# A decoder kernel whose first self attention gets half-row transposes and masks, fewer PSUM banks, its layer normalisation on ScalarE and its sine product on GpSimd

## The chip, the cores and the metric

The kernel runs on one core of one Trainium2 chip. The metric is device microseconds of one execution; the time of a kernel is the median of its runs.

## The reference, cut to what matters

A decoder of four layers runs over 32 sequences of 128 tokens and 128 features. The change touches only the first self attention of the first layer. What it computes, for x of 32 x 128 x 128:

```python
q, k = x @ W_Q + b_Q, x @ W_K + b_K            # 32 heads of 32
v = x @ W_V + b_V                              # 256 heads of 1: 8 per attention head
q, k = x_rot * cos + flip(x_rot) * sin         # rotary, over all 32 dimensions of a head
s = [virtual_k ; k] . q / sqrt(32)             # 16 virtual keys in front of 128, causal
p = softmax(s)
z = p @ [virtual_v ; v]
x = layernorm(x + z @ W_O)
```

`flip(a, b) = (-b, a)` swaps the halves of a head.

## The kernel before, in words

`l0_attn` (from L161) works in rounds. A round n handles eight heads of one sequence: NR = 4 rounds make a sequence, N = 128 rounds the stage. Two sequences share one projection, so eight rounds make a pair; `TAKE` lists which projections of the next pair are due in which of the eight rounds: X (the transposed input), K0 and Q0, K1, V and Q1, K2, Q2, K3, Q3. Those of the first pair run ahead of the loop (`FIRST`).

TensorE (L316 to L331) does in round n, in this order: `weights_T` (L278) for the first six of nine 128x128 blocks of round n-2's softmax weights, `scores(n)` (L260), the last three blocks, the projections due (`produce`, L237), and `mix` (L287), which multiplies the transposed weights of round n-2 with the virtual values (L298) and the values (L300). `scores` first writes the causal mask into each of four score banks, by a product of an identity with the mask in bf16 (L271), the first two banks after half of the previous round's subtractions, the other two after all of them; then it adds 8 products of 32 rows for keys and queries (L275). Every fourth round `project` (L304) runs ahead of the masks. PSUM has eight banks: 0 to 3 hold the scores, 4 and 5 form a ring that transposed weights and projections share in the order written out at `order`, and 6 and 7 hold the mixed values of two rounds each, in turn (`z_of`).

VectorE (L484 on) does the softmax's maximum (L458), every fourth round the residual (L453), the values once in a pair (L440), and the subtractions (L467, L471). Behind them come in even rounds `normalise` (L482), in odd rounds `spread` (L476), and in some rounds `turn` (L447), the product of the half-swapped keys and queries with the sine. Every 16 rounds the layer normalisation of four sequences follows: statistics (L68, L72) and two rounds later `dve_ln_scale` (L124).

ScalarE (L388 on) copies the transposed weights to SBUF in three pieces of 384 (`weights`, L384), takes the exponential (L395), evacuates projections with their bias (`take`, L359 and L369), and inverts the softmax sums (`invert`, L375 and L377).

GpSimd (L405 on) handles a quarter q of a pair's keys and queries at a time: two products with the cosine (L422), then, when the sine product is there, two additions (L427). SP swaps the half heads with eight DMAs per quarter (L342).

Of the kernel before, what the change touches and what calls it, by code (L numbers as in the profile page):

```python
# [9 lines left out]
ALU = mybir.AluOpType  # L10
# [6 lines left out]
P = 128  # L17
# [109 lines left out]

def dve_ln_affine(nc, dve, E, s, k, src, dst, scale, shift):
# [35 lines left out]
def l0_attn(nc, E):  # L164
# [22 lines left out]
    with sublayer(nc, "cst vkc one xt_ps xt kq_ps raw flip0 flip1 cosm sinm rot v_ps v s_ps mx sub_a sub ex pt_ps pt z_ps shuf lnz rz zt o_ps res" + LN) as (s, ctx):  # L187
# [8 lines left out]
        MASK = ctx.enter_context(nc.sbuf_tensor(f"maskb_{nc.next_id()}", [P, 2, K], BF16))  # L196
# [3 lines left out]
        order = [(item, 0) for item in FIRST]  # L200
        for n in range(N + 2):
            if n >= 2:
                order += [("T0", n - 2), ("T1", n - 2), ("T2", n - 2)]
            order += due(n)
        place = {item: k for k, item in enumerate(order)}

        def ring(item, n):
            return PS[:, 4 + place[item, n] % 2, :]

        def ring_free(pe, item, n):  # L210

            k = place[item, n] - 2
            if k < 0:
                return
            before, m = order[k]
            if before[0] == "T":
                pe.wait_ge(s.pt, 3 * m + int(before[1]) + 1)
            elif before == "X":
                pe.wait_ge(s.xt, m + 1)
            elif before == "V":  # L220
                pe.wait_ge(s.v, m + 1)
            else:
                pe.wait_ge(s.raw, 8 * m + 2 * int(before[1]) + (before[0] == "Q") + 1)

        def z_of(m):
            return PS[:, 6 + m % 2, 0:2 * P].rearrange("p (r q) -> p r q", r=2)
# [6 lines left out]
        def o_of(t):  # L233
            return PS[:, 0, 384:384 + P]

        with nc.Block() as block:
            @block.tensor  # L237
            def _(pe):
                def produce(item, p):
                    bank = ring(item, p)  # L240
                    ring_free(pe, item, p)
# [17 lines left out]
                def scores(n):  # L259
# [6 lines left out]
                    if n >= 2 * NR and n % NR == 0:  # L266
                        project(n // NR - 2)
# [11 lines left out]
                def weights_T(n, c):  # L279
                    item = f"T{c}"  # L280
                    if c == 0:
                        pe.wait_ge(s.ex, n + 1)
                    ring_free(pe, item, n)
                    for q in range(3):
                        ins = nc.tensor.transpose(ring(item, n)[:, q * P:(q + 1) * P], SM[:, n % 3, 3 * c + q, :], E.ident)  # L285
                    ins.then_inc(s.pt_ps, 1)

                def mix(n, a):
                    r, t, m = n % NR, n // NR, n // 2
                    p, b = t // PB, t % PB  # L290
                    z = z_of(m)[:, r % 2]
                    pe.wait_ge(s.pt, 3 * n + 2 + a)
                    if a == 0:
                        if n % NPR == 0:
# [18 lines left out]
                for item in FIRST:  # L313
                    produce(item, 0)
                for n in range(N + NR + 1):
                    live = 2 <= n < N + 2  # L316
                    if live:
                        weights_T(n - 2, 0)
                        weights_T(n - 2, 1)
                    if n < N:  # L320
                        scores(n)
                    elif n % NR == 0:
                        pe.wait_ge(s.sub, N)
                        project(n // NR - 2)
                    if live:
                        weights_T(n - 2, 2)
# [20 lines left out]
            def _(act):  # L347
                nc.scalar.preload_act_table_set(EXP_LN)

                def take(item, p):  # L350
                    if item == "V":
                        return
                    bank = ring(item, p)
# [25 lines left out]
                def weights(k):  # L379
# [3774 lines left out]
```

## Time and profile before

| | us |
|---|---|
| median of 3 runs | 3554.46 (3548.69 to 3561.56) |
| profiled execution | 3553.89 |
| its span | 3552.0 |
| first self attention, about | 71 to 742 of the span |

Busy shares of the span: TensorE 78%, its weight loads 56%, VectorE 69%, ScalarE 55%, GpSimd 44%. The page's chain of waits covers the end of the kernel, far from the stage that changes, so the stage is read by its own windows, timelines and waits. Its reductions (L458) come once a round and serve as a clock of the rounds.

### The profile page before, as it was taken

How to read it: one execution, taken by the hardware profiler on the slowest of the kernel's cores; microseconds unless marked ns; L12 is line 12 of the kernel's file. 1: busy time of each engine (PE TensorE's matmuls, PEld its weight loads, DVE VectorE, ACT ScalarE, POOL GpSimd, SP SyncE). 2: the span in 40 equal slices, each digit the busy share in tenths (PEclk: the TensorE clock that was granted, in tenths of full speed). 3: DMA queues.
4: the chain of work that ended last, by engine and by line, in shares of the span. 5: the costliest groups of instructions: out<-in, count | busy, mean ns of one | idle time of the engine just before them, and what ended most of it. 6: DMA issues, size and time to landing. Idle time of an engine off the chain costs nothing. (4 is left out here: it accounts for less than half of the span.)

```text
span 3552.0 us, 78931 instructions
## 1 busy us (share of the span) xinstructions
PE 2759.6 (78%) x29371; PEld 1989.7 (56%) x29371; DVE 2452.4 (69%) x7164; ACT 1962.8 (55%) x3803; POOL 1547.7 (44%) x1205
## 2 busy tenths in 40 slices
PE   2899999987875957989899999956655657868956
PEld 1677777655564845656455555534433447745646
DVE  6688888865555967976676776659882544568955
ACT  2677777744443854765555655555433724556637
POOL 3554555412237823520165555623231258815544
PEclk9999999999966978989999999977767858979958
DMA  4333333212202211000000000000007012300013
GB/s 137 56 55 55 55 55 55 49 60 79 69 18 63 76 50 66 2 1 1 1 2 3 2 3 2 3 1 19 19 27 219 12 44 66 103 26 12 2 32 100
DMA packets 103272, 151.01 MB, mean 43 GB/s; under 512 B 26266, under 2 KB 76524, under 8 KB 101756
## 3 DMA queue, kind: packets, MB, share of 16 engines
q1 hardware_dynamic: 91546, 123.11, 13.9%
q0 software_dynamic: 10912, 22.70, 1.9%
q8 instruction: 237, 3.88, 0.5%
q14 instruction: 143, 1.17, 0.1%
q10 hardware_dynamic: 434, 0.15, 0.0%
HBM read 81.13 MB, written 49.04 MB: 37 GB/s over the span
## 5 line engine op out<-in xcount | busy, mean ns | idle before, releaser
L458 DVE TENSOR_REDUCE MX<-banks 128x8 f32<-128x1152 f32 x128 | 173.2, 1353 | 101.3 <-PE banks L275 101.2
L2450 POOL TENSOR_TENSOR SM<-SM,RZ 128x1232 f32<-128x1232 f32 x64 | 143.8, 2247 | 190.0 <-DVE RZ L2492 188.9
L1727 POOL DMA_INDIRECT expert_results<-Y,DST x181 | 177.8, 982 | 81.5 <-DVE DST L1910 33.8
L427 POOL TENSOR_TENSOR KT<-KT,FL 128x512 f32<-128x512 f32 x64 | 81.6, 1276 | 302.0 <-DVE FL L447 302.0
L1714 POOL DMA_INDIRECT sorted_rows<-SRC,IDX x160 | 156.7, 979 | 128.7 <-DVE IDX L1843 82.1
L1496 PE MATMUL banks<-XC,WR 128*128 128x128 f32 x1448 | 197.4, 280 | 0.3 <-ACT XC L1616 0.2
L384 ACT COPY PT<-banks 128x384 f32<-128x384 f32 x384 | 170.3, 478 | 47.3 <-PE banks L285 43.6
L2434 ACT COPY PT<-banks 77x512 f32<-77x512 f32 x256 | 143.0, 583 | 86.2 <-PE banks L2353 83.3
L285 PE MATMUL banks<-sb_c_ident,SM 128*128 128x128 f32 x1152 | 182.7, 286 | 9.8 <-ACT PT L384 9.3
L1496 PEld LDWEIGHTS banks<-XC,WR 128*128 128x128 f32 x1448 | 180.8, 196 | 2.6 <-ACT XC L1616 1.9
L2790 POOL TENSOR_TENSOR KQ<-T,EX 128x1024 f32<-128x1024 f32 x32 | 76.1, 2379 | 208.4 <-ACT EX L2771 208.4
L471 DVE TENSOR_TENSOR SM<-banks,MX 128x512 f32<-128x512 f32 x256 | 163.6, 680 | 0.0
L2353 PE MATMUL banks<-sb_c_ident,SM 128*77 128x128 f32 x1024 | 160.2, 291 | 0.1
L1506 PE MATMUL banks<-WR,HT 128*128 128x128 f32 x1008 | 149.3, 282 | 5.7 <-DVE HT L1949 3.3
L395 ACT ACTIVATE SM<-SM 128x1152 f32<-128x1152 f32 x128 | 150.4, 1175 | 4.9 <-DVE SM L471 4.2
L285 PEld LDWEIGHTS banks<-sb_c_ident,SM 128*128 128x128 f32 x1152 | 121.5, 141 | 55.8 <-issue 25.7
L2353 PEld LDWEIGHTS banks<-sb_c_ident,SM 128*77 128x77 f32 x1024 | 114.8, 151 | 53.6 <-issue 40.0
L369 ACT ACTIVATE RAW<-banks,weight_region 128x256 f32<-128x256 f32 x256 | 108.0, 477 | 63.4 <-PE banks L256 53.9
L256 PE MATMUL banks<-XT,weight_region 128*128 128x256 f32 x512 | 135.8, 395 | 4.6 <-ACT RAW L369 4.0
L1506 PEld LDWEIGHTS banks<-WR,HT 128*128 128x128 f32 x1008 | 127.1, 192 | 13.5 <-DVE HT L1949 7.4
L59 PE MATMUL banks<-sb_c_ident,x_res 128*128 128x128 f32 x256 | 47.4, 329 | 112.0 <-PEq L48 112.0
L1635 ACT ACTIVATE HT<-banks,WR 128x128 f32<-128x128 f32 x284 | 81.5, 368 | 95.7 <-PE banks L1496 91.2
(566 smaller groups left out, 8597.9 us busy)
## 6 DMA issues: line engine op xcount, KB each, us to landing
FL<-RAW SPq DMA_DIRECT2D x512, 64.0 KB, 2.3
sorted_rows<-in_zeros_dram SPq DMA_DIRECT2D x33, 528.0 KB, 8.6
XR<-sorted_rows SPq DMA_DIRECT2D x181, 66.0 KB, 1.9
SRC<-expert_results SPq DMA_DIRECT2D x16, 512.0 KB, 7.5
T<-s4d_k_dram SPq DMA_DIRECT2D x8, 1024.0 KB, 10.0
weight_region<-in_l_ffn__wall_dram SPq DMA_DIRECT2D x1, 4112.0 KB
film_dram<-F SPq DMA_DIRECT2D x8, 512.0 KB, 2.9
FO<-film_dram SPq DMA_DIRECT2D x8, 512.0 KB, 4.7
```

The source lines that it names most:

```text
L285: ins = nc.tensor.transpose(ring(item, n)[:, q * P:(q + 1) * P], SM[:, n % 3, 3 * c + q, :], E.ident)
L384: nc.scalar.copy(PT[:, n % 2, 3 * c:3 * c + 3, :].rearrange("p h q -> p (h q)"), ring(f"T{c}", n)[:, 0:3 * P]).then_inc(s.pt, 1)
L395: nc.scalar.activation(SM[:, (n - 1) % 3], SM[:, (n - 1) % 3], ACT.Exp, scale=SCALE).then_inc(s.ex, 1)
L458: nc.vector.tensor_reduce(MX[:, n % 2], sc, AXX, ALU.max).then_inc(s.mx, 1)
L471: nc.vector.tensor_tensor(main[:, h:h + 2], sc[:, h:h + 2, :, 0:P], bc(MX[:, n % 2, h:h + 2].unsqueeze(3), [P, 2, 2, P]), ALU.subtract).th ...
L1496: ins = nc.tensor.matmul(up_bank(j, c // 2)[:, (c % 2) * P:(c % 2 + 1) * P], w[:, at * P:(at + 1) * P], XC[:, j % 2, :], start=True, stop= ...
L1506: ins = nc.tensor.matmul(down_bank(j), HT[:, j % 2, c, :], w[:, c * P:(c + 1) * P], start=c == 0, stop=c == hb - 1)
L1714: nc.gpsimd.indirect_dma_start(out=rows, out_offset=bass.IndirectOffsetOnAxis(ap=IDX[:, k, t:t + 1], axis=0), in_=SRC[:, t, k, :], in_offs ...
L1727: nc.gpsimd.indirect_dma_start(out=results, out_offset=bass.IndirectOffsetOnAxis(ap=DST[:, j % ST:j % ST + 1], axis=0), in_=Y[:, j % ST, : ...
L2353: ins = nc.tensor.transpose(bank_of("T", k)[0:L, c * P:(c + 1) * P], SM[:, t % 3, 4 * c + a, :], E.ident)
L2434: nc.scalar.copy(PT[:, t % 2, a].rearrange("p c q -> p (c q)"), bank_of("T", k)[0:L, :]).then_inc(s.pt, 1)
L2450: nc.gpsimd.tensor_tensor(SM[:, t % 3], SM[:, t % 3], bc(RZ[:, t % 2, :].unsqueeze(2), [P, H, L]), ALU.mult).then_inc(s.nm, 1)
```

## The change

- The masks and the transposes work on half rows: a transpose loads 64 partitions and streams 64 columns, 16 of them per round in place of 8 full ones, into two banks (`turned`, banks 4 and 5); the virtual keys' block stays a full transpose, into bank 7. The masks are eight products of 64x64 in place of four.
- ScalarE copies the transposed weights in one piece of 1024 and one of 128, and inverts the sums between its copies and its exponential.
- There is no ring: of the projections due the first goes to bank 7, the second to bank 4, after ScalarE's copies of the round; the next transposes wait until they are taken. `project` moves behind the scores and those copies, and writes bank 5.
- One bank holds mixed values (6), so `mix` of an even round waits for `normalise`, which moves between VectorE's reduction and its subtractions.
- The layer normalisation is applied by ScalarE (four activations with scale and shift per partition) after a small product on VectorE.
- The sine product moves from VectorE to GpSimd, between the cosine products and the additions.

```diff
+def dve_ln_shift(nc, dve, E, s, k):
+    dve.wait_ge(s.ln_rstd, k + 1)
+    nc.vector.scalar_tensor_tensor(E.ln_std[k % 8][:], E.ln_rstd[k % 8][:], -1.0, E.ln_mv[k % 8][:, :, 0], ALU.mult, ALU.mult).then_inc(s.ln_core, 1)
+def act_ln_apply(nc, act, E, s, k, src, dst):
+    shift, rstd = E.ln_std[k % 8], E.ln_rstd[k % 8]
+    act.wait_ge(s.ln_core, k + 1)
+    for b in range(GB):
+        ins = nc.scalar.activation(dst[:, b, :], src[:, b, :], ACT.Identity, bias=shift[:, b:b + 1], scale=rstd[:, b:b + 1])
...
+        turned = PS[:, 4:6, :].rearrange("p r (h q) -> p h r q", q=64)
+        turned_vk = PS[:, 7, 0:P]
+        z_bank = PS[:, 6, 0:2 * P].rearrange("p (r q) -> p r q", r=2)
...
-                        nc.tensor.matmul(PS[:, i, 0:2 * K], IDB[:], MASK[:].rearrange("p a k -> p (a k)"), start=True, stop=False)
+                        at = HALF[i % 2]
+                        for late in range(2):
+                            nc.tensor.matmul(PS[HALF[late], i, 0:2 * K], IDB[at, at], MASK[at, late].rearrange("p a k -> p (a k)"), start=True, stop=False)
...
+                def weights_T(n):
+                    pe.wait_ge(s.ex, n + 1)
+                    if n >= 1:
+                        pe.wait_ge(s.pt, 2 * n)
+                    if n + 1 >= 2 * NR and (n + 1) % NR == 0:
+                        pe.wait_ge(s.res, (n + 1) // NR - 1)
+                    new = due(n + 1) if n >= 1 else [(item, 0) for item in FIRST] + due(0) + due(1)
+                    for item, p in new[1:]:
+                        taken(pe, item, p)
+                    for k in range(8):
+                        for r in range(2):
+                            ins = nc.tensor.transpose(turned[:, k, r, :], SM[HALF[r], n % 3, 1 + k, :], E.ident[HALF[r], HALF[r]])
                     ins.then_inc(s.pt_ps, 1)
+                    for item, p in new[:1]:
+                        taken(pe, item, p)
+                    nc.tensor.transpose(turned_vk, SM[:, n % 3, 0, :], E.ident).then_inc(s.pt_ps, 1)
...
-                        if n % 2 == 0 and m >= 2:
-                            pe.wait_ge(s.zt, m - 1)
+                        if n % 2 == 0 and m >= 1:
+                            pe.wait_ge(s.zt, m)
...
                     if live:
-                        weights_T(n - 2, 0)
-                        weights_T(n - 2, 1)
+                        weights_T(n - 2)
                     if n < N:
                         scores(n)
+                    if live:
+                        pe.wait_ge(s.pt, 2 * (n - 2) + 2)
...
+                    if n >= 2 * NR and n % NR == 0:
                         project(n // NR - 2)
-                    if live:
-                        weights_T(n - 2, 2)
...
+                    nc.scalar.copy(PT[:, n % 2, 1:9, :].rearrange("p h (r q) -> p h r q", r=2), turned).then_inc(s.pt, 1)
+                    act.wait_ge(s.pt_ps, 2 * n + 2)
+                    nc.scalar.copy(PT[:, n % 2, 0, :], turned_vk).then_inc(s.pt, 1)
...
+                    pool.wait_ge(flips[q % 2], 128 * (q // 2 + 1))
+                    f = FL[:, q % 2].rearrange("p a j (b q) -> p (a j b) q", b=PB)
+                    nc.gpsimd.tensor_tensor(f, f, bc(E.sin.unsqueeze(1), [P, 8, P]), ALU.mult).then_inc(s.sinm, 1)
...
+                    if n >= 4 and n % 2 == 0:
+                        normalise((n - 4) // 2)
                     dve.wait_ge(s.mx, n + 1)
...
-                        dve_ln_scale(nc, dve, E, s, g, grp(E.x, g), grp(E.x, g))
+                        dve_ln_shift(nc, dve, E, s, g)
```

## Rows read from the trace of the kernel before

**Rows 1.** Windows: start:end us, length, busy PE, PEld, DVE, ACT, POOL, PEclk, DMA, GB/s.
```profile
300.00:400.00 100.00, 94.58 (x1094) 72.89 (x1095) 83.12 (x145) 72.82 (x148) 48.31 (x39) 1.00 0.33 54
```

**Rows 2.** Timeline, 300 to 325 us: start, length, engine, line, operation, operands, count.
```profile
299.36 1.35 DVE L458 TENSOR_REDUCE MX<-banks 128x8 f32<-128x1152 f32 x1
...
300.63 0.28 DVE L453 TENSOR_TENSOR x_res<-banks,x_res 128x128 f32<-128x128 f32 x1
...
302.22 0.41 DVE L482 TENSOR_TENSOR ZT<-banks,RZ 128x256 f32<-128x256 f32 x1
...
302.55 1.22 DVE L447 TENSOR_TENSOR FL<-FL,sb_f_sin 128x1024 f32<-128x1024 f32 x1
...
303.79 1.89 PE L256 MATMUL banks<-XT,weight_region 128*128 128x256 f32 x8
...
304.86 1.70 ACT L369 ACTIVATE RAW<-banks,weight_region 128x256 f32<-128x256 f32 x4 [0.39 <-PE banks L256]
...
308.55 1.36 DVE L458 TENSOR_REDUCE MX<-banks 128x8 f32<-128x1152 f32 x1 [1.54 <-PE banks L275]
...
308.79 1.04 PE L256 MATMUL banks<-XT,weight_region 128*128 128x256 f32 x4
...
309.67 0.38 PE L298 MATMUL banks<-PT,sb_l_attn__vv 128*128 128x128 f32 x2
...
309.99 0.65 PE L300 MATMUL banks<-PT,VZ 128*32 128x128 f32 x16
...
310.15 1.28 DVE L471 TENSOR_TENSOR SM<-banks,MX 128x512 f32<-128x512 f32 x2
...
310.56 0.88 PE L285 MATMUL banks<-sb_c_ident,SM 128*128 128x128 f32 x6
...
311.27 0.65 PE L271 MATMUL banks<-maskb,identb 128*128 128x288 bf16 x4
...
311.86 0.77 PE L275 MATMUL banks<-KT,QT 32*128 32x144 f32 x16
...
312.70 1.36 DVE L458 TENSOR_REDUCE MX<-banks 128x8 f32<-128x1152 f32 x1 [0.94 <-PE banks L275]
```

**Rows 3.** Timeline of VectorE: reductions of rounds 0, 120 and 127.
```profile
91.41 1.36 DVE L458 TENSOR_REDUCE MX<-banks 128x8 f32<-128x1152 f32 x1 [4.78 <-PE banks L275]
...
694.69 1.35 DVE L458 TENSOR_REDUCE MX<-banks 128x8 f32<-128x1152 f32 x1
...
725.68 1.36 DVE L458 TENSOR_REDUCE MX<-banks 128x8 f32<-128x1152 f32 x1 [1.53 <-PE banks L275]
```

**Rows 4.** Waits, 130 to 690 us: us in total, times, longest us.
```profile
PEld banks L275 <- issue: 27.1, 114, 0.2
...
DVE FL L447 <- DMA FL<-RAW: 21.3, 15, 2.8
```

**Rows 5.** Timeline of TensorE in a later stage with half-row transposes (L2644).
```profile
1902.89 0.71 PE L2644 MATMUL banks<-sb_c_ident,T 64*128 64x64 f32 x16
1903.53 1.09 PE L2654 MATMUL banks<-LA,sb_a_gla_sum 64*64 64x512 f32 x8
```

**Rows 6.** Groups by line and form, whole span: busy us, mean ns, idle before and releaser.
```profile
L2747 ACT COPY T2T<-banks 128x1024 f32<-128x1024 f32 x32 | 32.7, 1022 | 0.8 <-PE banks L2644 0.8
...
L2426 ACT COPY ZT<-banks 128x128 f32<-128x128 f32 x64 | 16.0, 250 | 3.1 <-PE banks L2366 3.1
...
L1660 ACT ACTIVATE x_res<-x_res,FNM,FRS 128x128 f32<-128x128 f32 x96 | 39.0, 479 | 2.5 <-DVE FNM L1987 2.5
...
L422 POOL TENSOR_TENSOR KT<-RAW,sb_f_cos 128x512 f32<-128x512 f32 x64 | 81.4, 1272 | 4.5 <-ACT RAW L369 4.5
...
L2790 POOL TENSOR_TENSOR KQ<-T,EX 128x1024 f32<-128x1024 f32 x32 | 76.1, 2379 | 208.4 <-ACT EX L2771 208.4
```

**Rows 7.** Instructions of the half-swap tile, ns min/median/max; then DMA issues, us to landing.
```profile
L342 SPq DMA_DIRECT2D FL<-RAW x512: 507/589/1892, 78.2 to 694.4; - x171
...
FL<-RAW SPq DMA_DIRECT2D x512, 64.0 KB, 2.3
```

More of the change, by code:

```diff
@@ L195, in l0_attn, with bank_of, taken @@
         RZ = sb("RZ", [P, 2, 2, P]); ZT = sb("ZT", [P, 4, 2, P])
-        MASK = ctx.enter_context(nc.sbuf_tensor(f"maskb_{nc.next_id()}", [P, 2, K], BF16))
+        MASK = ctx.enter_context(nc.sbuf_tensor(f"maskb_{nc.next_id()}", [P, 2, 2, K], BF16))
         IDB = ctx.enter_context(nc.sbuf_tensor(f"identb_{nc.next_id()}", [P, P], BF16))
         flips = (s.flip0, s.flip1)
[L200 to L221, printed above, removed]
-            else:
-                pe.wait_ge(s.raw, 8 * m + 2 * int(before[1]) + (before[0] == "Q") + 1)
-        def z_of(m):
-            return PS[:, 6 + m % 2, 0:2 * P].rearrange("p (r q) -> p r q", r=2)
+        HALF = (slice(0, 64), slice(64, 128))
+        def bank_of(item, p):
+            if p == 0:
+                return PS[:, 4 + FIRST.index(item) % 2, :]
+            return PS[:, 4 if [row for row in TAKE if item in row][0].index(item) else 7, :]
+        def taken(pe, item, p):
+            if item == "X":
+                pe.wait_ge(s.xt, p + 1)
+            elif item == "V":
+                pe.wait_ge(s.v, p + 1)
+            else:
+                pe.wait_ge(s.raw, 8 * p + 2 * int(item[1]) + (item[0] == "Q") + 1)
+        turned = PS[:, 4:6, :].rearrange("p r (h q) -> p h r q", q=64)
+        turned_vk = PS[:, 7, 0:P]
+        z_bank = PS[:, 6, 0:2 * P].rearrange("p (r q) -> p r q", r=2)
         def value_window(p, b, r, i, a):
@@ L239, in produce @@
                 def produce(item, p):
-                    bank = ring(item, p)
-                    ring_free(pe, item, p)
+                    bank = bank_of(item, p)
                     if item == "X":
@@ L312, in _ @@
                 pe.wait_ge(s.vkc, 2)
-                for item in FIRST:
+                for k, item in enumerate(FIRST):
+                    if k >= 2:
+                        taken(pe, FIRST[k - 2], 0)
                     produce(item, 0)
@@ L352, in take @@
                         return
-                    bank = ring(item, p)
+                    bank = bank_of(item, p)
                     if item == "X":
@@ L390, in _ @@
                     if live:
-                        weights(3 * (n - 2))
-                        weights(3 * (n - 2) + 1)
+                        weights(n - 2)
+                    if n >= 4 and n % 2 == 0 and (n - 4) // 2 < HALVES:
+                        invert((n - 4) // 2)
                     if 1 <= n <= N:
@@ L430, in _ @@
             def _(dve):
-                nc.vector.tensor_copy(MASK[:], bc(E.causal.unsqueeze(1), [P, 2, K]))
+                for a in range(2):
+                    nc.vector.tensor_copy(MASK[:, :, a], E.causal)
                 nc.vector.tensor_copy(IDB[:], E.ident).then_inc(s.cst, 1)
@@ L491, in _ @@
                         residual(n // NR - 2)
-                    if n >= 4 and n % 2 == 0 and (n - 4) // 2 < HALVES:
+                    if n >= N and n % 2 == 0 and (n - 4) // 2 < HALVES:
                         normalise((n - 4) // 2)
@@ L4127, in shape_constants @@
     c["f_sin"] = np.tile(np.sin(angle) * sign, (4, 1)).astype(f)
[L4128 removed]
+    c["f_causal"] = np.where(np.arange(P + 16)[None, None] <= p[:, :, None] % 64 + 64 * np.arange(2)[None, :, None] + 16, 0, -1e30).astype(f)
     same = p // 64 == q // 64
```

54 lines of the change are left out of this document (16 added, 38 removed).

## Prediction

> **What bounds the kernel now.** Only the first self attention is touched, so I read first where it lies. The windows of 100 us show TensorE busy for 94.6 of 100 us there, at a granted clock of 1.00, the 2.4 GHz level, with no other engine above 83 [rows 1]. A busy TensorE need not be the limit, so I went to the timeline of two rounds. In the round that starts with the reduction at 308.55, TensorE's groups follow each other without a gap: projection of one item 0.88 (308.79 to 309.67), virtual values 0.32, mixing 0.57, six transposes 0.71, four masks 0.59, then the scores, whose next reduction starts 0.84 after they do [rows 2]. The score banks close a second loop of the same length: reduction to end of the subtractions 2.88 (308.55 to 311.43), then 1.27 to the next reduction: 4.15 us in all. So in a plain round TensorE's order and the score banks bind together. Rounds with two projected items, an output projection or VectorE's product with the sine are longer, and the mean from the first reduction to that of round 120 is (694.69 - 91.41)/120 = 5.03 us [rows 3]. VectorE also stands still 21.3 us, 15 times, because the product with the sine waits in its queue for the half-swapped copies [rows 4]; whoever is behind it (the next reduction, hence TensorE's masks) waits too.
>
> **The change, part by part.**
> TensorE: nine full transposes cost 0.71/6 = 0.12 us each. Sixteen half ones exist elsewhere in this kernel in the same form, 64x128 loaded and 64 columns streamed: from their start to the next group it takes 0.64, and 0.71 to their last result [rows 5]. I take that row; the far bound is eight full transposes, 0.94, if the loads of the two halves did not run side by side. The remaining full transpose costs 0.12 and a change of tile shape 0.11 (that is 0.59 for four masks less four streams of 288 columns, 0.12 each), together 0.23. The eight quarter masks use four separate tiles, so four run abreast: 2 x 0.12 and 0.11 to the scores, 0.35 instead of 0.59; bounds 0.35 and 0.59. TensorE's own work in a plain round falls by about 0.45 us.
>
> But the banks are fewer: one pair of banks for the transposes, one for the mixed values instead of two. That adds two waits, and they set the new rounds.
>
> Even rounds. Mixing now waits for the normalisation of the same round, which VectorE runs behind the reduction. Loop: 1.27 (reduction until the next instruction, 299.36 to 300.63), normalisation 0.41, a hand-over of 0.05 (estimate), virtual values 0.32, mixing 0.57, half transposes 0.64, the full one 0.23, masks 0.35, scores to reduction 0.84: 4.68 us [rows 2, 5]. Every fourth round VectorE adds the residual in front, 0.20 (its 0.28 less 0.08, by which the instruction behind the reduction overlaps too): 4.88. Queued behind the waiting mixing on TensorE is the whole next round; behind the normalisation on VectorE are the subtractions.
>
> Odd rounds with one item. The score banks: 2.88, hand-over 0.05, two masks' time 0.12, change 0.11, scores 0.84: 4.00.
>
> Odd rounds with two items (K0/Q0, V/Q1). The next transposes wait until ScalarE has taken both: 0.71 transposes, hand-over 0.06, the copy of 1024 elements 1.02, of the last 128 another 0.15 (0.25 less the 0.10 by which ScalarE's instructions overlap), 0.05, projection of two items 1.89 to its end (303.79 to 305.68), ScalarE 0.88 after it (to 306.56), 0.05: 4.81 [rows 2, 6]. The unknown is the copy's stride over two banks: 1.02 by the nearest row, a contiguous copy of the same size; 1.3 as far bound, were it eight copies of 0.25 with the overlap.
>
> Eight rounds: 4.88 + 4.81 + 4.68 + 4.81 + 4.88 + 4.00 + 4.68 + 4.00 = 36.74; sixteen: 73.5.
>
> Normalisation of the layer on ScalarE, once in 16 rounds. VectorE loses its four normalising instructions, which I count as no gain of their own, since the new loops already hold only what stays. ScalarE gains four of 0.48 [rows 6], about 1.64 with overlap, and they are in front of the next round's copies. They wait for VectorE's small product, which comes after that round's subtractions and shuffle, about 3.4 us after its reduction (2.88 and two short instructions, estimate). So the copies start at 3.4 + 0.06 + 1.64 = 5.1 and end at 6.3; the output projection needs them and takes about 1.0 to its result (estimate: the 0.88 of one projected item and the end of the pipeline): 7.4 with the hand-over. The residual behind the reduction could otherwise begin at 4.00 + 1.27 = 5.3. The round grows by 2.1; bounds 0, if ScalarE had room, and 3. Sixteen rounds: 75.6.
>
> The product with the sine on GpSimd. VectorE spends 1.22 on it [rows 2], GpSimd by the nearest row of 1024 elements 2.38 (bounds VectorE's 1.22 and twice GpSimd's 1.27), so a quarter pair keeps GpSimd busy for 4 x 1.27 + 2.38 = 7.5 us [rows 6], against about 9 us between two of them. Its path: SP issues eight transfers at 0.59, landing takes 2.3, 7.0 us [rows 7], then 2.38 and two additions: 11.9 from raw values to rotated ones. The tightest deadline is the last quarter, three rounds (14.4 us) later. So it is hidden in steady state, and if that cover of 2.5 us goes, every pair of sequences pays. In the first four rounds it is not hidden: they follow GpSimd's chain, 7.5 us each, and the first starts 1.2 later. The wait for the half-swapped copies moves from VectorE's queue to GpSimd's, where only the next quarter is behind it.
>
> **Sum.** Reduction 0 to reduction 120: 3 x 7.5, then 4.81 + 4.68 + 4.00 + 4.68 + 4.00 (no output projection yet), then 7 x 75.6: 573.9 against 603.3 [rows 3], -29.4. First reduction +1.2. The last seven intervals, 31.0 before [rows 3]: 7.0 + 4.0 + 4.7 + 4.0 + 4.9 + 4.0 + 4.7 = 33.3, +2.3. End of the stage, ScalarE's four instructions after one more hand-over: +1. That is -25. For what such a sum leaves out (the layer statistics, which stay on VectorE, and waits that add up by chance) I put back 0.06 us a round, 8 us. Net -17 from the profiled execution's 3553.89, which lies 0.6 below the median of the runs: **3537 us**.
>
> **Rivals.**
> *Tile shapes (slower).* TensorE changes its tile shape six times a round instead of four. Each round now shows 0.24 us without a weight load before the scores (27.1 us in 114 rounds, put down to issue) [rows 4], right behind the masks, while the streaming itself shows only 0.11 lost. If nothing of an added change overlaps, it costs 0.24 and an exposed load of 0.14, 0.27 more than I took; two of them, in the 12 of 16 rounds whose loop runs through the transposes and in half of that in the others, make 0.54 x 112 = 60 us: 3597. It decides from 0.13 more per change on (28 us), where the time passes 3565. For it: the load gap in every round. Against it: the half transposes' row, 0.64 to the next group, already holds one such change. The Trainium skill, TensorEngine Tiling (Array Packing), section Key Properties, says that a change of tiling mode, not of the tile alone, drains TensorE; it speaks for this rival. By that rule at its full price the time would be that 3597; by the row, 3537.
> *ScalarE late (no change).* One set of transposition banks ties ScalarE's copies, its four normalisations and the takes into one loop. With the copy at 1.2 instead of 1.02 the two-item rounds, and the rounds after a layer normalisation, lengthen by 0.18 and some plain odd ones too, and if the takes land 0.1 later every odd round pays: some 13 us, 3550. For it: ScalarE becomes the engine in four of eight rounds' loops. Against: even rounds hide it.
> *GpSimd late (no change or slower).* Should the path of 11.9 take over 14.4, each of the 15 later pairs waits by the excess; 2 us over give 30, 3567. Against: half the path is transfers of steady length.
> *More gain.* If the layer normalisation finds room (7 x 2.1) and the 8 us are not needed: 3514.
>
> **How the numbers follow.** About 0.3%, 10.7 us, is what a measurement of this kernel can tell from no change. Forecast 0.56 (almost all of it faster), more gain 0.07, ScalarE late 0.20, tile shapes 0.12, GpSimd late 0.05. Faster 0.61, same 0.21, slower 0.18. The range reaches from 3519 (the normalisations hidden) to 3566, where the tile shapes begin to decide; the forecast's own is 3525 to 3548.
>
> **What would show it.** Right: reductions 4.7 to 4.9 apart in even rounds, with the normalisation between reduction and subtractions and TensorE idle until it ends; 4.0 in plain odd rounds; one round in sixteen near 7; half transposes at 0.64 to the next group; the first rounds 7.5 apart. Wrong: half transposes near 0.94; a gap of 0.3 or more at the full transpose or the quarter masks; scores waiting for GpSimd's additions in the fourth round of a pair; a granted clock below 1.00 in the stage, for which no row here gives a reason.

## The result: the changed kernel is slower, and the profile after

| | before | after |
|---|---|---|
| median of 5 runs, us | 3554.62 (3548.69 to 3561.56) | 3585.49 (3581.99 to 3590.26) |
| profiled execution, its span | 3553.89, 3552.0 | 3585.49, 3583.5 |
| first reduction of the stage | 91.41 [rows 3] | 96.04 |
| last reduction of the stage | 725.68 [rows 3] | 749.17 |

The ratio is 1.0089 (95% interval 1.0074 to 1.0105): 0.9% slower, 48 us above the forecast and above its range. Nearly all of it lies in the stage that was changed: the next one begins at 770.9 instead of 742.3. Busy shares of the span: TensorE 77%, its weight loads 55%, VectorE 66%, ScalarE 55%, GpSimd 47%.

The first thing to read is the column PEclk of the windows. The stretch that showed 94.58 us of TensorE at a clock of 1.00 [rows 1] shows less work and less clock (columns: window, length, busy PE, PEld, DVE, ACT, POOL, PEclk, DMA share, GB/s):

```profile
300.00:400.00 100.00, 88.17 (x1196) 63.78 (x1192) 61.57 (x119) 66.31 (x122) 69.98 (x49) 0.90 0.30 50
```

The reductions (now L473) are the clock of the rounds again. An ordinary pair of sequences has the intervals 5.10, 5.00, 4.91, 5.00, 5.11, 4.02, 4.91 and 4.02: 38.07 us against the 36.74 predicted, still less than the 38.7 to 40.5 of before. Once in 16 rounds, though, one round stands out. After the seven layer normalisations on ScalarE that fall inside the loop, the round (24, 40, 56, 72, 88, 104 and 120) takes 10.15, 10.02, 9.44, 10.95, 9.82, 7.11 and 10.14 us, where 7.0 was predicted, and the round behind it takes 5.7 to 6.8 in five of six cases, where others of its place take 5.00. The timeline of round 56 (start us, length, engine, line, operation, operands, count, idle before and releaser):

```profile
383.84 0.15 DVE L131 SCALAR_TENSOR_TENSOR ln_std<-ln_rstd,ln_mv 128x4 f32<-128x4 f32 x1
...
384.02 1.65 ACT L139 ACTIVATE x_res<-x_res,ln_std,ln_rstd 128x128 f32<-128x128 f32 x4 [1.44 <-DVE ln_std L131]
384.72 1.36 DVE L473 TENSOR_REDUCE MX<-banks 128x8 f32<-128x1152 f32 x1 [0.73 <-PE banks L280]
...
385.58 0.99 ACT L398 COPY PT<-banks 128x1024 f32<-128x1024 f32 x1
...
386.78 1.38 PE L321 MATMUL banks<-weight_region,ZT 128*128 128x128 f32 x8 [2.13 <-ACT PT L400]
...
388.19 0.29 DVE L468 TENSOR_TENSOR x_res<-banks,x_res 128x128 f32<-128x128 f32 x1 [2.12 <-PE banks L321]
388.96 0.77 PE L311 MATMUL banks<-PT,sb_l_attn__vv 128*128 128x128 f32 x2 [0.38 <-DVE ZT L499]
...
390.67 1.11 PE L295 MATMUL banks<-sb_c_ident,SM 64*128 64x64 f32 x16
...
394.16 1.36 DVE L473 TENSOR_REDUCE MX<-banks 128x8 f32<-128x1152 f32 x1 [3.95 <-PE banks L280]
```

The wait is the predicted one: four activations of 1.65 behind VectorE's small product and ahead of the copies, and TensorE's output projection (L321) waits 2.13 us for those copies. What was not predicted comes behind it. Windows of 2 us over the same stretch:

```profile
384.00:386.00 2.00, 0.65 (x16) 0.43 (x16) 1.28 (x1) 1.98 (x5) 2.00 (x2) 1.00 0.63 100
386.00:388.00 2.00, 1.22 (x9) 1.22 (x10) 0.07 (x1) 1.97 (x5) 1.58 (x2) 0.89 0.63 102
388.00:390.00 2.00, 1.62 (x13) 1.01 (x15) 1.80 (x5) 0.92 (x2) 0.66 (x1) 0.50 0.22 35
...
396.00:398.00 2.00, 2.00 (x7) 1.54 (x5) 1.04 (x2) 1.00 (x3) 0.00 (x0) 0.55 0.00 0
398.00:400.00 2.00, 1.84 (x42) 1.26 (x41) 0.45 (x2) 1.11 (x3) 1.24 (x1) 1.00 0.13 18
```

TensorE works 0.65 us of 2.00, then the granted clock goes to 0.50, which is 1.2 GHz, and stays there until about 397. Everything on TensorE's path takes longer meanwhile: the sixteen half transposes 1.11 instead of 0.71, and so on.

The start of the stage also differs. TensorE begins at 76.29 instead of 72.50, because it waits for the cast of the identity, which lasts 3.63 us beside GpSimd's clearing of the value tile. In the kernel before, the same cast began ahead of the clearing and took 0.42. First the kernel before, then the changed one:

```profile
72.02 0.42 DVE L432 CAST identb<-sb_c_ident 128x128 bf16<-128x128 f32 x1
...
72.50 0.68 PE L244 MATMUL banks<-sb_c_ident,x_res 128*128 128x128 f32 x2 [7.06 <-DVE identb L432]
```

```profile
72.46 3.70 POOL L425 MEMSET VZ<- 128x4128 f32 x1
72.60 3.63 DVE L452 CAST identb<-sb_c_ident 128x128 bf16<-128x128 f32 x1
...
76.29 0.69 PE L249 MATMUL banks<-sb_c_ident,x_res 128*128 128x128 f32 x2 [10.68 <-DVE identb L452]
```

At the end, where no projections are left to fill TensorE, the clock falls as well; from the last reduction to the next stage it takes 21.7 us (749.17 to 770.90) instead of 16.7 (725.68 to 742.38):

```profile
748.00:756.00 8.00, 6.37 (x59) 4.75 (x59) 3.83 (x8) 4.05 (x7) 0.00 (x0) 0.50 0.00 0
756.00:764.00 8.00, 5.07 (x54) 3.37 (x54) 0.86 (x3) 2.01 (x4) 0.00 (x0) 0.50 0.01 3
```

The product with the sine is where the prediction put it. Of the waits between 130 and 690 us (engine, line, waited for: us, times, longest), these two answer to [rows 4]; no wait of TensorE for GpSimd is among those of 5 us or more:

```profile
POOL FL L442 <- DMA FL<-RAW: 129.1, 56, 5.6
...
PE banks L321 <- ACT PT L400: 15.3, 6, 3.2
```

### The profile page after: what moved, and what is told of

The parts are those of the page before. It is cut to its first block and busy times, and to the rows that moved or that the text cites. A ratio compares the mean times of both kernels' runs of the same rounds, so it can differ in the third digit from the quotient of the medians.

```text
span 3583.5 us, 81910 instructions
## 1 busy us (share of the span) xinstructions
PE 2754.9 (77%) x30907; PEld 1963.4 (55%) x30907; DVE 2366.2 (66%) x7077; ACT 1960.9 (55%) x3707; POOL 1698.5 (47%) x1269
## 5 line engine op out<-in xcount | busy, mean ns | idle before, releaser
L473 DVE TENSOR_REDUCE MX<-banks 128x8 f32<-128x1152 f32 x128 | 173.5, 1356 | 216.5 <-PE banks L280 216.4
L442 POOL TENSOR_TENSOR FL<-FL,sb_f_sin 128x1024 f32<-128x1024 f32 x64 | 151.4, 2365 | 138.5 <-DMA FL<-RAW 138.5
L398 ACT COPY PT<-banks 128x1024 f32<-128x1024 f32 x128 | 129.4, 1011 | 146.6 <-PE banks L295 146.6
L261 PE MATMUL banks<-XT,weight_region 128*128 128x256 f32 x512 | 147.5, 420 | 4.6 <-ACT RAW L384 4.0
L2644 PE MATMUL banks<-weight_region,XT 128*64 128x512 f32 x512 | 125.1, 610 | 2.2 <-DVE LA L2844 2.2
L1497 PE MATMUL banks<-sb_c_ident,XR 128*128 128x128 f32 x181 | 50.9, 281 | 92.6 <-DMA XR<-sorted_rows 92.5
```

What stands on the lines that cost most here:

```text
L261: ins = nc.tensor.matmul(bank[:, jj * PTOK:(jj + 1) * PTOK], w[:, j * P:(j + 1) * P], XT[:, p % 2, :], start=True, stop=True)
L442: nc.gpsimd.tensor_tensor(f, f, bc(E.sin.unsqueeze(1), [P, 8, P]), ALU.mult).then_inc(s.sinm, 1)
L473: nc.vector.tensor_reduce(MX[:, n % 2], sc, AXX, ALU.max).then_inc(s.mx, 1)
```

## The experiments

The theory after reading the traces: ScalarE's normalisations ahead of the copies leave TensorE idle for 2 us, and the fall of the clock behind that is what costs; without it the change would be faster. Rival 1: the product with the sine on GpSimd costs. Rival 2: the half-row transposes and quarter masks cost. All ratios are to the kernel before, with 95% intervals.

**e4_busy: keep TensorE at work during the wait.** Every wait of the changed kernel stays; TensorE only gets work that nobody needs.

```diff
+                    if GB * NR + 8 <= n < N and (n - 8) % (GB * NR) == 0:
+                        pe.wait_ge(s.shuf, (n - 4) // 2 + 1)
+                        for _ in range(16):
+                            ins = nc.tensor.transpose(PS[:, 6, 256:384], E.ident, E.ident)
+                        ins.then_inc(s.fill, 1)
                     if live:
                         pe.wait_ge(s.pt, 2 * (n - 2) + 2)
...
                     dve.wait_ge(s.rz, m + 1)
+                    if m >= 10 and (m - 2) % 8 == 0 and m < N // 2 - 2:
+                        dve.wait_ge(s.fill, (m - 2) // 8)
```

> The changed kernel with sixteen extra full transposes of the identity on TensorE, behind the scores of the round after each normalisation, into an unused half of the mixed values' bank, so that TensorE has some 1.9 us of work where it stood idle for 2.1. ScalarE's order and all waits stay. Theory (wait and clock apart): the wait alone makes that round 7.0 to 7.3 us, the clock the rest; with TensorE busy the clock stays at 1.00, the round takes 7.0 to 7.5 instead of 10, the one after it 5.0, the time is 3553 to 3566. Rival (the wait alone is the loss, and the clock only follows): the round stays at 9 or more and the time above 3578.

Measured: 3561.51 us, ratio 1.0024 (1.0011 to 1.0038), 24 us less than the changed kernel, by adding work, and still 0.2% more than the kernel before. Six of the seven rounds take 7.10 to 7.91, the one behind each 4.99 to 5.01; only the last, next to the rounds without projections, still takes 9.27. The same round as above, and the window of 300 to 400 us:

```profile
375.04 1.65 ACT L139 ACTIVATE x_res<-x_res,ln_std,ln_rstd 128x128 f32<-128x128 f32 x4 [1.44 <-DVE ln_std L131]
...
375.59 1.97 PE L339 MATMUL banks<-sb_c_ident 128*128 128x128 f32 x16
375.73 1.36 DVE L478 TENSOR_REDUCE MX<-banks 128x8 f32<-128x1152 f32 x1 [0.73 <-PE banks L280]
...
377.79 1.16 PE L321 MATMUL banks<-weight_region,ZT 128*128 128x128 f32 x8 [0.24 <-ACT PT L405]
...
382.83 1.36 DVE L478 TENSOR_REDUCE MX<-banks 128x8 f32<-128x1152 f32 x1 [1.83 <-PE banks L280]
```

```profile
300.00:400.00 100.00, 91.57 (x1345) 67.31 (x1343) 67.59 (x131) 72.38 (x132) 73.70 (x51) 1.00 0.33 53
```

Up to the output projection the two rounds are the same but for the added transposes: it starts 2.06 us behind the reduction in both (386.78 - 384.72, 377.79 - 375.73). From there this one takes 5.04 us to its end and the changed kernel's 7.38. So in this round the wait is worth 2.0 us (7.10 less the ordinary 5.11) and the clock 2.3 more (9.44 less 7.10), with 1.8 in the next round (6.78 less 5.00). Over all seven the rounds take 67.6 us in the changed kernel and 53.8 here, the six behind them 35.8 and 30.0: the clock costs 13.8 + 5.8 = 19.6 us in the loop, and most of the 24. Shown: the two are separate, and the clock follows what TensorE does during the wait. The theory is too strong in one point, though: with the clock kept, the waits that are left still hold the change above the kernel before. The rounds of 7.5 to 7.9 have a longer small product on VectorE (L131), which takes 0.15 us in some rounds and up to 1.2 in others; what runs beside it is told at the end.

**e3_ln_spread: the normalisation stays on ScalarE, but behind the next round's work.** Two of the four activations follow the takes of the next round, two those of the round eight later.

```diff
-                    if n >= GB * NR + 7 and (n - GB * NR - 7) % (GB * NR) == 0:
-                        g = (n - GB * NR - 7) // (GB * NR)
-                        act_ln_apply(nc, act, E, s, g, grp(E.x, g), grp(E.x, g))
+                    for late in (8, 16):
+                        g = (n - GB * NR - late) // (GB * NR)
+                        if g >= 0 and g < NB // GB - 1 and (n - late) % (GB * NR) == 0:
+                            act_ln_part(nc, act, E, s, g, grp(E.x, g), grp(E.x, g), (late // 8 - 1) * 2)
+                    if n == N + 7:
+                        act_ln_apply(nc, act, E, s, NB // GB - 1, grp(E.x, NB // GB - 1), grp(E.x, NB // GB - 1))
```

> The changed kernel with the layer normalisation still on ScalarE, but two of its four activations behind the takes of the next round and two eight rounds later (the last group's four stay where they are). Theory: nothing stands ahead of the copies any more, no round of the loop is longer than 5.6, the clock keeps 1.00 from about 150 us on, and the time is 3538 to 3552, faster than both kernels. Rival (the clock falls in this stage for another reason, such as the quarter masks' and half transposes' smaller share of the array): windows at 0.90 to 0.95 remain and the time stays above 3565.

Measured: 3547.08 us, ratio 0.9978 (0.9965 to 0.9992), 38 us less than the changed kernel and 0.2% less than the one before. The seven rounds take 5.10 or 5.11. ScalarE does its two activations, and the next copy still finds the engine waiting for TensorE:

```profile
373.58 0.88 ACT L148 ACTIVATE x_res<-x_res,ln_std,ln_rstd 128x128 f32<-128x128 f32 x2
375.70 1.01 ACT L406 COPY PT<-banks 128x1024 f32<-128x1024 f32 x1 [1.24 <-PE banks L303]
```

```profile
300.00:400.00 100.00, 92.17 (x1379) 67.41 (x1375) 69.42 (x133) 74.41 (x136) 76.80 (x52) 1.00 0.34 55
```

Behind 687 us, in the rounds without projections, the clock still falls. The theory holds up to there, with the wait gone as well as the fall, and rival 2 falls as the cause of the loss: half transposes and quarter masks are all still there. No run measures their price apart.

**e1_ln_vector: the normalisation back on VectorE.**

```diff
-                    if n >= GB * NR + 7 and (n - GB * NR - 7) % (GB * NR) == 0:
-                        g = (n - GB * NR - 7) // (GB * NR)
-                        act_ln_apply(nc, act, E, s, g, grp(E.x, g), grp(E.x, g))
...
-                        dve_ln_shift(nc, dve, E, s, g)
+                        dve_ln_scale(nc, dve, E, s, g, grp(E.x, g), grp(E.x, g))
```

> The changed kernel with the layer normalisation applied by VectorE again, as before the change; all else stays. Theory (the loss is ScalarE's four normalisations ahead of the next round's copies, which leave TensorE idle for over 2 us and are followed by a granted clock of 0.50 for 8 to 10 us): the round after each normalisation falls from about 10 to 5.5 to 6.5 us, the windows of the stage stand at a granted clock of 0.97 or more, and the time is 3585 less seven times about 5 and less some of the stage's end, 3545 to 3557. Rival 1 (the sine product on GpSimd) and rival 2 (half-row transposes and quarter masks): ordinary rounds carry the loss, the round after the normalisation gives back 2 us at most, the time stays above 3570.

Measured: 3585.72 us, ratio 1.0103 (1.0074 to 1.0131). The expectation was wrong by 29 us, and with it my theory's first form, in which ScalarE was the culprit; by the time alone the rivals would stand, and it takes the timeline and e3_ln_spread to tell. On VectorE the same piece of work harms as much: the round that holds it takes 6.2 to 8.0 us where 4.02 is ordinary, and the next one 6.5 to 7.2. The timeline shows why:

```profile
380.25 4.10 DVE L124 TENSOR_SCALAR x_res<-x_res,ln_mv,ln_rstd 128x128 f32<-128x128 f32 x4
...
380.29 1.26 POOL L443 TENSOR_TENSOR QT<-QT,FL 128x512 f32<-128x512 f32 x1
...
381.51 1.28 POOL L435 TENSOR_TENSOR KT<-RAW,sb_f_cos 128x512 f32<-128x512 f32 x1
...
382.75 1.26 POOL L435 TENSOR_TENSOR QT<-RAW,sb_f_cos 128x512 f32<-128x512 f32 x1
...
384.27 1.34 DVE L470 TENSOR_REDUCE MX<-banks 128x8 f32<-128x1152 f32 x1
...
386.29 0.77 PE L311 MATMUL banks<-PT,sb_l_attn__vv 128*128 128x128 f32 x2 [3.92 <-DVE ZT L496]
```

The four normalising instructions, 0.33 us each at their shortest, last 4.10 together, beside three of GpSimd's. The reduction behind them is late, the normalisation of the mixed values behind that, TensorE waits 3.92 us for it, and the clock is 0.50 in the next window of 2 us (386 to 388). So it is not ScalarE as such: from either engine the normalisation makes TensorE wait. In the kernel before, the same instructions cost 0.95 us (5.71 in the round that holds them, 4.76 in others of its place), presumably since mixing did not wait for the same round's normalisation; that was not tried.

**e8_before_ln_scalar: ScalarE's normalisation alone, in the kernel before.**

```diff
                         act_rstd(nc, act, E, s, (n - GB * NR - 6) // (GB * NR))
+                    if n >= GB * NR + 7 and (n - GB * NR - 7) % (GB * NR) == 0:
+                        g = (n - GB * NR - 7) // (GB * NR)
+                        act_ln_apply(nc, act, E, s, g, grp(E.x, g), grp(E.x, g))
...
-                        dve_ln_scale(nc, dve, E, s, g, grp(E.x, g), grp(E.x, g))
+                        dve_ln_shift(nc, dve, E, s, g)
```

> The kernel before with one thing changed: its layer normalisation is applied by ScalarE, with VectorE's small product, at the end of the same round as in the changed kernel. Theory A (it is the placement ahead of the copies that hurts, in either order of rounds): the round after each normalisation grows by 2 to 5, TensorE idles there and the clock falls, the time is 3565 to 3590. Theory B (with two banks of mixed values and a ring of transposition banks the order before has the slack for it; the harm comes from the new order's fewer banks): rounds stay within 1 us of before and the time is 3548 to 3560.

Measured: 3565.11 us, ratio 1.0025 (1.0015 to 1.0035), at the lower edge of theory A but not by its mechanism. Six of seven rounds after a normalisation take 5.62 instead of 4.33 and the next 0.13 more. The seventh takes 7.19, and there the clock does fall (0.57 from 622 to 626 us). That makes 6 x 1.42 + 3.0, some 11.5 us. The round ahead of them, rid of VectorE's four instructions, takes 4.76 instead of 5.71, which gives back 7 x 0.95 = 6.6: some 5 us net. The rest of the 9 lies in rounds 0 to 7 (53.3 us against 51.3) and behind the loop, and is not explained. In the six, TensorE waits 1.40 us ahead of its last three transposes and the clock stays at 1.00:

```profile
382.25 0.55 PE L300 MATMUL banks<-sb_c_ident,SM 128*128 128x128 f32 x3 [1.40 <-ACT PT L399]
...
386.54 1.36 DVE L476 TENSOR_REDUCE MX<-banks 128x8 f32<-128x1152 f32 x1 [1.21 <-PE banks L290]
```

Neither theory is right as it stands. The placement ahead of the copies costs in either kernel; the old order pays almost only for a shorter wait and gets most of it back on VectorE, the new one pays for a longer wait and the clock.

**e2_sine_vector and e7_spread_sine_vector: the product with the sine back on VectorE,** in the changed kernel and in e3_ln_spread, at the places that it had before.

```diff
-                    pool.wait_ge(flips[q % 2], 128 * (q // 2 + 1))
-                    f = FL[:, q % 2].rearrange("p a j (b q) -> p (a j b) q", b=PB)
-                    nc.gpsimd.tensor_tensor(f, f, bc(E.sin.unsqueeze(1), [P, 8, P]), ALU.mult).then_inc(s.sinm, 1)
...
+                    if n < NR:
+                        turn(n)
...
+                    if n // NPR + 1 < NP and n % NPR in (3, 5, 6):
+                        turn(NR * (n // NPR + 1) + (3, 5, 6).index(n % NPR))
+                    if n >= NPR and n // NPR < NP and n % NPR == 0:
+                        turn(NR * (n // NPR) + 3)
```

> The changed kernel with the sine product on VectorE again, at its old places; all else stays. Theory: GpSimd's product is hidden in steady state, so moving it back gains nothing there and puts four instructions of 1.2 us per pair into VectorE's queue: rounds after a normalisation still take about 10 us at a clock of 0.50, the first four rounds are some 1 us shorter each, others get longer by 0 to 1.2, the time is 3580 to 3625. Rival 1 (the sine product on GpSimd is what costs): the time falls to 3550 or less.

> The kernel of e3_ln_spread with the sine product on VectorE again, at its old places: the price of that move with the clock kept. Theory: the rounds that hold the product and the wait for the half-swapped copies are longer, 39.6 us in eight instead of 38.1, and the rounds after a normalisation lose 0 to 2 us, 25 to 35 us in the stage; no round above 7 between rounds 8 and 119; the time is 3568 to 3585, so the move to GpSimd is worth about that. Rival (VectorE has room in the new order, since its subtractions only follow the normalisation): 38.1 to 38.5 in eight rounds, the time within 8 of e3_ln_spread's.

Measured: 3613.44 us, ratio 1.0170 (1.0145 to 1.0196), and 3593.47, ratio 1.0111 (1.0096 to 1.0127). The first is inside its range, but its first four rounds are 2.4 us longer together where shorter ones were expected, and the rounds after a normalisation take 7.6 to 10.9. Rival 1 falls: the move to GpSimd saves 28 us in the changed kernel (3613.4 - 3585.5) and 46 where the normalisation is out of the way (3593.5 - 3547.1). The second is more than the 25 to 35 expected. Its undisturbed eight rounds take 39.6 us, as expected, but most take 40 to 43 (with one round of 7.29, where none above 7 was expected), and the windows of 100 us from 200 to 700 stand at a clock of 0.95 to 0.97: VectorE's longer queue makes TensorE wait (up to 2.3 us), and most of the longer waits are followed by the lower clock too.

**e11_rebuilt_alone: both moves undone,** the edits of e1_ln_vector and e2_sine_vector together.

> The changed kernel without the two moves of the title: layer normalisation and sine product both on VectorE, the rebuilt rounds alone. Theory (VectorE's normalising instructions are stretched by GpSimd's instructions beside them, and GpSimd has a third less to do without the sine product): the four take less than the 4.1 us of e1_ln_vector and about the 2.7 of the kernel before. The product on VectorE costs some 46 us against GpSimd, as between e7 and e3, and the normalisation stands in the same queue as in e1_ln_vector: 3610 to 3640. Rival (the stretch has nothing to do with GpSimd): the four still take 4.0 or more in the mean.

Measured: 3607.49 us, ratio 1.0132 (1.0110 to 1.0154), a little below what was expected. The four normalising instructions per layer normalisation between 130 and 690 us (24 in all: busy us, mean ns), first in e1_ln_vector, then here, where GpSimd has a third less to do:

```profile
L124 DVE TENSOR_SCALAR x_res<-x_res,ln_mv,ln_rstd 128x128 f32<-128x128 f32 x24 | 24.5, 1079 | 0.0
```

```profile
L124 DVE TENSOR_SCALAR x_res<-x_res,ln_mv,ln_rstd 128x128 f32<-128x128 f32 x24 | 14.9, 681 | 0.0
```

And in the kernel before:

```profile
L124 DVE TENSOR_SCALAR x_res<-x_res,ln_mv,ln_rstd 128x128 f32<-128x128 f32 x24 | 15.9, 722 | 0.0
```

The stretch goes with GpSimd's load, as the theory had it. The rebuilt rounds by themselves are thus some 50 us slower than the kernel before, and the two moves of the title give back 22 as they are placed and 60 with e3_ln_spread's placement. How the 50 divide between fewer banks, VectorE's queue and the clock (0.91 to 0.97 from 200 to 700 us) was not measured apart.

**e6_spread_start and e10_ident_first: the start.** The first moves TensorE's wait for the masks and the bf16 identity behind the first projections, which need neither; the second also casts the identity ahead of the masks.

```diff
-                pe.wait_ge(s.cst, 1)
-                pe.wait_ge(s.vkc, 2)
                 for k, item in enumerate(FIRST):
...
                     produce(item, 0)
+                pe.wait_ge(s.cst, 1)
+                pe.wait_ge(s.vkc, 2)
```

```diff
+                nc.vector.tensor_copy(IDB[:], E.ident)
                 for a in range(2):
-                    nc.vector.tensor_copy(MASK[:, :, a], E.causal)
-                nc.vector.tensor_copy(IDB[:], E.ident).then_inc(s.cst, 1)
+                    ins = nc.vector.tensor_copy(MASK[:, :, a], E.causal)
+                ins.then_inc(s.cst, 1)
```

> The kernel of e3_ln_spread, and TensorE's wait for the masks and the bf16 identity moves from ahead of the first projections to ahead of the first scores. Theory (the identity's cast falls beside GpSimd's clearing of 128x4128 and lasts 3.63 us instead of 0.42, and TensorE waits for it): TensorE starts at about 72.5 instead of 76.3, the first reduction comes at 92.2 to 92.6 instead of 95.8, the time is 3.5 us less than that of e3_ln_spread, 3541 to 3546. Rival (the first quarter's chain of GpSimd starts no earlier, because its clearing has to end first): the first reduction stays above 94.

> The kernel of e6_spread_start with the identity's cast ahead of the two casts of the mask. Theory (a VectorE cast from SBUF to SBUF that meets GpSimd's clearing of 128x4128 lasts as long as the clearing, whatever it casts): the identity's cast, now at the start, takes 0.4 us, and the mask's second cast, now beside the clearing, takes more than 3. Rival (it is the identity's cast itself that is slow, by its operand): the identity takes 3.6 again and the masks' two casts together 1.0 as before. The time is that of e6_spread_start either way.

Measured: 3543.60 us, ratio 0.9965 (0.9952 to 0.9979), first reduction at 92.25 instead of 95.80; and one run of 3543.28, first reduction at 92.34. In the second the slow cast is another one:

```profile
71.61 0.47 DVE L462 CAST identb<-sb_c_ident 128x128 bf16<-128x128 f32 x1 [4.92 <-PEq L48]
...
72.00 4.14 DVE L464 CAST maskb<-sb_f_causal 128x288 bf16<-128x288 f32 x2
72.28 3.70 POOL L437 MEMSET VZ<- 128x4128 f32 x1
```

So it is the meeting with GpSimd's clearing, not the operand, and the 3.6 us at the start are paid by whoever waits for that cast.

**e9_spread_start_fill: the last rounds kept busy as well,** on top of e6_spread_start: extra transposes before the mixing of the last even rounds, and similar ones at the end of the stage.

```diff
+                    if N - 6 <= n < N and n % 2 == 0:
+                        for _ in range(7 if n % NR == 0 else 14):
+                            nc.tensor.transpose(PS[:, 7, 128:256], E.ident, E.ident)
...
+                    if N <= n < N + 3:
+                        pe.wait_ge(s.sub, N)
+                        for _ in range(14 if n == N + 2 else 7):
+                            nc.tensor.transpose(PS[:, 0, 384:512], E.ident, E.ident)
```

> The kernel of e6_spread_start, and extra full transposes of the identity in the last six rounds that have no projections and at the end of the stage (14 or 7 at a place, into unused columns of banks), where TensorE stands idle for 0.8 to 2 us and the clock falls to 0.50. Theory: rounds 122 and 126 fall from 7.0 and 5.7 to 5, the last projection runs at 2.4 GHz, the stage ends 4 to 6 us earlier, the time is 3535 to 3541 and is faster than before by 0.4 to 0.5%. Rival (the extra work is itself in the way): the rounds stay where they are, the time equals that of e6_spread_start.

Measured: 3537.77 us, ratio 0.9954 (0.9940 to 0.9968), the fastest of all. Rounds 122 and 126 take 4.91 each (5.80 and 7.03 in e6_spread_start), and the clock holds until 716. From the last reduction to the next stage it takes 17.7 us (706.74 to 724.41), against 21.7 in e6_spread_start:

```profile
708.00:716.00 8.00, 5.83 (x82) 4.69 (x81) 2.58 (x8) 5.02 (x9) 0.00 (x0) 1.00 0.01 3
```

## Why the prediction was wrong

**The terms of the sum against the changed kernel's trace.**

| term | predicted, us | measured | missed by |
|---|---|---|---|
| first reduction | +1.2 | 96.04 - 91.41 = +4.6 | 3.4 |
| rounds 0 to 7 | 44.7 | 46.6 | 2.0 |
| seven times sixteen rounds, without the normalisations | 7 x 73.5 = 514.5 | 535.5 (the same rounds of e3_ln_spread) | 21.0 |
| the normalisations in them | 7 x 2.1 = 14.7 | 568.1 - 535.5 = 32.5 | 17.8 |
| last seven intervals | 33.3 | 749.17 - 710.76 = 38.4 | 5.1 |
| from the last reduction to the next stage | 16.7 + 1 | 21.7 | 4.0 |
| rest of the kernel | 0 | 2812.6 - 2809.7 = +3.0 | 3.0 |
| allowance | 8 | in the rows above | -8 |

Together 48, the distance from 3537 to 3585. Three rows need a word. Rounds 0 to 2 were priced rightly (7.39, 6.77 and 8.03 for three times 7.5); the miss there is round 3, 6.58 for 4.81, at a clock of 0.76 from 118 to 125 us. Rounds 8 to 119 hold six rounds after a normalisation, not seven: the seventh is round 120, which the last seven intervals have once more at 7.0. The sum thus counted one too many, and for the six, 12.6 stands against 32.5. The 3.0 in stages that were not touched are not explained.

**Right.** The bounds of the new rounds are the ones predicted: reduction, normalisation, mixing, transposes and scores in even rounds, score banks in plain odd ones (4.02 against 4.00), ScalarE's takes in two-item rounds. The prices hold: half transposes 0.64 to the next group, quarter masks 0.37 (0.35), copy of 1024 over two banks 1.01 (1.02), sine product on GpSimd 2.36 (2.38). That the product is hidden in steady state held as well, so *GpSimd late* did not come, and *tile shapes* neither: the change at the full transpose shows 0.26 instead of 0.23. *ScalarE late* had the right engine, at a place that I had priced in the sum.

**Failed: "The round grows by 2.1; bounds 0, if ScalarE had room, and 3."** The wait is right: e4_busy puts it at 2.0, or up to 2.8 where the small product is slow, and round 104 of the changed kernel, the one that kept its clock, takes 7.11 against 7.0. But the step ended with the wait and asked nothing of what TensorE does after having stood idle. By e4_busy the 32.5 us of the six rounds and those behind them are some 14 of wait and 19 of clock. The last part of the prediction named a clock below 1.00 as something "for which no row here gives a reason"; seen from the result, the reason was in its own sum, 2 us without work on TensorE once in 16 rounds. Six of seven such rounds paid for it, with 0.7 to 1.8 more in the next. The stage itself gave no warning: in the kernel before, TensorE stands idle there for 1.5 to 2.0 us four times between 130 and 690 us, and the clock stays at 1.00 (0.66 us of work in the window from 414 to 416, as little as the 0.65 above). A later stage could have: from 1000 to 1100 us of the kernel before, TensorE works 56.9 of 100 us at a mean clock of 0.58. The last rounds and the end of the stage failed in the same way. Of the 5.1 us missed in the last seven intervals 3.1 are round 120 (10.14 for 7.0) and 1.5 are round 126 (6.18 for 4.7); kept busy in e9_spread_start_fill, round 126 takes 4.91, and the end of the stage takes the 17.7 that the sum had. With the clock kept in the loop and the wait gone, e3_ln_spread lands 10 us above the forecast; that e9_spread_start_fill lands on the forecast is chance, since it has an earlier start and added work that the sum did not price.

**Failed: "a hand-over of 0.05 (estimate)", and the even rounds of 4.68.** The rows of an ordinary even round:

```profile
400.94 1.36 DVE L473 TENSOR_REDUCE MX<-banks 128x8 f32<-128x1152 f32 x1 [1.74 <-PE banks L280]
...
402.21 0.41 DVE L499 TENSOR_TENSOR ZT<-banks,RZ 128x256 f32<-128x256 f32 x1
...
402.77 0.46 PE L311 MATMUL banks<-PT,sb_l_attn__vv 128*128 128x128 f32 x2 [0.83 <-DVE ZT L499]
...
403.16 0.65 PE L313 MATMUL banks<-PT,VZ 128*32 128x128 f32 x16
...
403.74 0.71 PE L295 MATMUL banks<-sb_c_ident,SM 64*128 64x64 f32 x16
...
404.38 0.33 PE L299 MATMUL banks<-sb_c_ident,SM 128*128 128x128 f32 x1
...
404.64 0.44 PE L276 MATMUL banks<-maskb,identb 64*64 64x288 bf16 x8
...
405.85 1.36 DVE L473 TENSOR_REDUCE MX<-banks 128x8 f32<-128x1152 f32 x1 [1.83 <-PE banks L280]
```

From VectorE's end (402.21 + 0.41) to TensorE's start it takes 0.15, not 0.05; the virtual values take 0.39 instead of 0.32 (their weight load begins at 402.74, behind the wait and 0.03 ahead of the product; where nothing is waited for it begins 0.2 ahead, 407.34 for 407.56); 0.01, 0.03 and 0.02 more at the mixing, the full transpose and the masks. That is 0.23 in each even round. In two-item rounds the hand-over to the transposes is 0.14 for 0.05, and the projection takes 1.99 for 1.89. A mean of 0.19 a round makes 21 us; the allowance of 0.06 a round covered a third of it. Some 2 of the 21 are the layer statistics that the allowance was meant for (38.4 in the eight rounds that hold them, 38.1 in others).

**Failed: "the first starts 1.2 later".** The step counted the sine product and overlooked that the mask's second cast pushes the identity's beside GpSimd's clearing; e6_spread_start and e10_ident_first settle it.

## What to carry to other kernels

Price a wait on TensorE's path twice: as a wait, and by what the rounds behind it cost at 1.2 GHz; here, in five of six cases, idle stretches of 2.1 to 3.2 us cost 5.5 to 6.7 each (9.44 + 6.78 against 5.11 + 5.00, and so on). If such a wait can't be removed, work that nobody needs can be cheaper than standing idle (24 us here, and 6 more in the last rounds and at the end of the stage), and a rare piece of work belongs behind the instructions that the critical engine waits for, in pieces. Before moving work to GpSimd, look at what VectorE runs from SBUF to SBUF beside it.

## What the runs showed of the hardware

In rounds that were busy otherwise, the granted clock fell to 0.50 behind idle stretches of 2.1 to 3.2 us in the changed kernel and of 2.9 to 4.9 in e1_ln_vector, and in e2_sine_vector, e7_spread_sine_vector and e11_rebuilt_alone also behind some of 1.0 to 2.5. It did not fall behind six of seven of 1.40 (e8_before_ln_scalar), nor behind the four of 1.5 to 2.0 in the kernel before. The same 2.13 us were followed by a fall in round 56 and by none in round 104 of the same execution. So the length of one stretch does not tell; what does was not tried and stays open. The Trainium skill, TensorE: Matmul & The Clock Gate, section What's actually happening, says that the clock depends on how busy TensorE has been of late; e4_busy agrees, with 3561.5 us where the idle kernel needs 3585.5.

Three kinds of VectorE instructions were stretched beside GpSimd: a cast from 0.42 to 3.63 us, the normalising ones from 0.33 to 1.39 (e1_ln_vector), and the small product of 128x4 from 0.15 to 1.22 in the changed kernel (0.84 in each of the seven rounds of e8_before_ln_scalar), while the subtractions that read PSUM kept their 0.68. One of the slow small products, in the changed kernel's timeline: it begins 0.06 us behind one of GpSimd's additions and ends with it, and ScalarE's normalisation waits 2.51 us for it where 1.44 is usual.

```profile
300.32 1.27 POOL L446 TENSOR_TENSOR KT<-KT,FL 128x512 f32<-128x512 f32 x1
300.38 1.22 DVE L131 SCALAR_TENSOR_TENSOR ln_std<-ln_rstd,ln_mv 128x4 f32<-128x4 f32 x1
...
301.64 1.65 ACT L139 ACTIVATE x_res<-x_res,ln_std,ln_rstd 128x128 f32<-128x128 f32 x4 [2.51 <-DVE ln_std L131]
```

The Trainium skill, SBUF — State Buffer, section Who interferes with whom, says that VectorE's fast modes for casts and for products with scalars use ports that GpSimd shares, and that whoever comes second waits for the whole instruction of the first. The 3.63 beside a clearing of 3.70 and the 4.10 beside three of GpSimd's products agree with it.
